# A megakernel's last expert group: weighted blocks added into two DRAM sums by accumulating indirect DMAs, with its down weights resident

## The reference, cut to what matters

```python
topk_idx, tw = _route(x, router_w, bias)                    # 4 of 16 experts for each token
combine = (one_hot(topk_idx, E) * tw[..., None]).sum(1)
y = jnp.einsum('etf,efd->etd', silu(x @ gate_w) * (x @ up_w), down_w)
routed = jnp.einsum('etd,te->td', y, combine)               # the weighted sum of a token's 4 rows
sh = silu(x @ sh_gate_w) * (x @ sh_up_w) @ sh_down_w        # two shared experts
x = x + tanh(g_ffn[1]) * (routed + sh)
```

## Time and profile before

| | us |
|---|---|
| median of the 3 runs (1596.46 to 1602.15) | 1599.17 |
| the profiled execution's own time | 1602.94 |
| its span, first to last instruction | 1601.1 |
| PE busy | 1303.0 (81%) |
| ACT busy | 1082.0 (68%) |
| DVE busy | 974.2 (61%) |
| POOL busy | 528.5 (33%) |

### The profile page before, as it was taken

How to read it: one execution, slowest core, us unless ns; L and a number is a source line. 1 busy time by engine, 2 the same in 40 slices (tenths; PEclk the granted TensorE clock), 3 DMA queues, 4 the chain that set the end, 5 groups by cost and what they waited for, 6 DMA issues and landing times.

```text
span 1601.1 us, 34625 instructions
## 1 busy us (share of the span) xinstructions
PE 1303.0 (81%) x11876; PEld 762.8 (48%) x11876; DVE 974.2 (61%) x2365; ACT 1082.0 (68%) x1781; POOL 528.5 (33%) x505
## 2 busy tenths in 40 slices
PE   6766777886789899988999899889997886888860
PEld 2211231352236554745475546544666575577650
DVE  7985466438843965498438864886467775223323
ACT  4999788967597799976987897768882431222220
POOL 1100111131553212326543445246424334503216
PEclk8987997988899999999999999999998997899985
DMA  7665403310122433453444554434346545579964
GB/s 210 217 197 119 86 1 95 77 53 27 67 86 61 132 95 78 116 124 107 139 109 123 146 148 111 133 97 149 95 126 189 147 119 147 165 192 232 257 171 119
DMA packets 228148, 202.55 MB, mean 127 GB/s; under 512 B 117099, under 2 KB 185875, under 8 KB 227987
## 3 DMA queue, kind: packets, MB, share of 16 engines
q1 hardware_dynamic: 203731, 155.24, 36.3%
q0 software_dynamic: 12288, 33.57, 6.5%
q10 hardware_dynamic: 11968, 11.54, 2.2%
HBM read 107.49 MB, written 67.63 MB: 109 GB/s over the span
## 4 chain that ended last, share of the span: by engine, by line
PE 45%; DVE 21%; ACT 21%; issue 7%; POOL 4%; DMA 1%; another core or an unknown queue 1%; POOLq 0%; SPq 0%; ACTq 0%; DVEq 0%
ACT tanh_tiles L1217 17%; PE psF L989 7%; PE psE L835 6%; PE psE L837 5%; PE psE L836 5%; PE psY L835 3%; PE psY L837 2%; PE psY L836 2%; PE psF L835 2%; POOL work L821 2%; DVE stats L1394 1%; PE psF L1156 1%; PE psF L837 1%; PE psF L841 1%; PE psF L836 1%
## 5 line engine op out<-in xcount | busy, mean ns | idle before, releaser
L1217 ACT ACTIVATE tanh_tiles<-feat,text_bias 128x512 f32<-128x512 f32 x1232 | 774.7, 714 | 76.6 <-DVE feat L1590 58.6
L989 PE MATMUL psF<-tanh_tiles,wslide 128*32 128x512 f32 x2464 | 374.5, 667 | 60.7 <-ACT tanh_tiles L1217 57.7
L1619 DVE TENSOR_TENSOR tile<-tile,psE 128x512 f32<-128x512 f32 x128 | 87.5, 684 | 159.8 <-ACT tile L1244 76.9
L768 POOL TENSOR_TENSOR hid<-tile,hid 128x512 f16<-128x512 f32 x76 | 88.4, 1163 | 251.2 <-ACT hid L1236 250.0
L821 POOL TENSOR_TENSOR work<-work 128x512 f16<-128x512 f32 (+1 forms) x80 | 95.5, 1197 | 228.0 <-DVE work L1756 228.0
L1236 ACT CAST hid<-tile 128x512 f16<-128x512 f32 x128 | 78.6, 614 | 133.5 <-DVE tile L1619 116.5
L792 POOL DMA_INDIRECT xs_rows<-xs,slot_i x128 | 127.2, 993 | 118.2 <-issue 32.0
L835 PE MATMUL psY<-down,hid 128*128 128x256 f16 x512 | 143.7, 281 | 18.4 <-issue 11.6
L836 PE MATMUL psE<-xg,up_hi 128*128 128x128 f16 x768 | 148.1, 222 | 9.5 <-issue 9.2
L837 PE MATMUL psE<-xg,up_lo 128*128 128x128 f16 x768 | 147.6, 221 | 9.7 <-issue 9.5
L835 PE MATMUL psE<-xg,up_hi 128*128 128x128 f16 x768 | 148.2, 221 | 6.9 <-issue 5.9
(11 more groups left out here) (302 smaller groups left out, 2880.9 us busy)
## 6 DMA issues: line engine op xcount, KB each, us to landing
down<-down_split SPq DMA_DIRECT2D x208, 256.0 KB
y_rows<-hid SPq DMA_DIRECT2D x52, 256.0 KB
xs_rows<-peakT SPq DMA_DIRECT2D x24, 512.0 KB, 6.8
y_rows<-tanh_tiles ACTq DMA_DIRECT2D x44, 256.0 KB
down_split<-hid SPq DMA_DIRECT2D x18, 256.0 KB, 3.4
xscan<-in_x SPq DMA_DIRECT2D x8, 512.0 KB, 5.2
x<-in_x SPq DMA_DIRECT2D x8, 512.0 KB, 5.4
w_lin<-w_split SPq DMA_DIRECT2D x15, 256.0 KB
```

The lines of the kernel that those rows point to most:

```text
L768: pool.tensor_tensor(hid_lo[:, n], tile[:, v.n % 2], hid_hi[:, n], ALU.subtract).then_inc(glo_done, 1)
L989: last = pe.matmul(psF[32 * j:32 * j + 32, RHO, :], wslide[:, c, 31 - g:63 - g], tanh_tiles[:, st.at(SETS, 2 * g + c) % HRING, j], start=g ...
L1217: act.activation(tanh_tiles[:, n % HRING, j], feat[:, c], ACT.Tanh, bias=text_bias[:, c, col:col + 1]).then_inc(h_ready, 1)
L1619: dve.tensor_tensor(tile[:, n], tile[:, n], psE[:, (2 * v.n + 1) % 3], ALU.mult).then_inc(g_done, 1)
```

## The change

It concerns group 3, the last one (`LASTG`), and nothing else of the arithmetic.

- The scattered rows become 1,120 bytes wide (`WIDE`): the two halves, the token's number and its 16 expert weights. They go to a DRAM table of their own, `xs_last`, which SP fills in steps 3 to 6 with empty rows that carry the number of one of 128 spare rows. Two sums in DRAM (`sums`, 1,152 rows of 256 fp32) are zeroed in step 7.
- One slot after a unit's start SP loads the numbers and weights of its 256 rows (`meta`). DVE picks, for each row, the weight of the block's owner (three small instructions, `wrow`).
- The copy of psY into the ring becomes two ACT instructions of 256 columns, scaled by `wrow`. The store to `y_rows` is gone.
- Instead, POOL adds block 0 of the unit into `sums[0]` 11 slots after the unit's start and block 1 into `sums[1]` one slot later, each with an indirect DMA that accumulates. Each waits for the one before into the same sum to have landed.
- At the end SP loads both sums in 8 DMAs of 256 KB, DVE adds them to `x` in 8 instructions of 512 columns, and SP stores 4 pieces. The 32 gathers and their weighted adds are gone.
- The down weights of the 16 experts are loaded once into SBUF (`resident`, 16 DMAs of 256 KB, step 9, slots 14 to 29), over buffers that the front part no longer needs. The 48 loads of a unit's own are gone; the down products now address `resident` by register.

```diff
+                if s == STEPS + 1 and 14 <= i < 14 + 1 * E and (i - 14) % 1 == 0:
+                    e = (i - 14) // 1
+                    if e == 0:
+                        sp.wait_ge(ids_ready, GROUPS)
+                        sp.wait_ge(slots_ready, GROUPS)
+                    sp.dma_start(resident[:, e].rearrange("p a k d -> p (a k d)"), down_dram[e]).then_inc(resident_loaded, 16)
...
             run(None, slot)
-            for c in range(CHUNKS):
-                sp.wait_ge(added, (GROUPS - 1) * CHUNKS + c + 1)
-                sp.dma_start(ov[2 * GROUPS - 2 + c // NT][:, c % NT], x[:, c // NT, c % NT]).then_inc(final_stored, 16)
+            sp.wait_ge(added, LASTG * CHUNKS)
+            for b in range(2):
+                sp.wait_ge(summed[b], 16 * NPAIR)
+            for q in range(4):
+                for b in range(2):
+                    rows = sums[b][2 * q * P:2 * (q + 1) * P].rearrange("(n p) c -> p n c", p=P)
+                    sp.dma_start(part[b][:, 2 * q:2 * q + 2], rows).then_inc(part_loaded[q], 16)
...
+                for b in range(2):
+                    v = began(T, STORE + b)
+                    if v and v.routed and v.g == LASTG:
+                        pool.wait_ge(y_kept, v.kept)
+                        if v.pair:
+                            pool.wait_ge(summed[b], 16 * v.pair)
+                        else:
+                            pool.wait_ge(last_filled, 16 * (PIECES + 2))
+                        keep_pace(i, s)
+                        pool.indirect_dma_start(sums[b], bass.IndirectOffsetOnAxis(ap=token_ids(v, b), axis=0),
+                                                y_rows(v)[:, b * D:(b + 1) * D], None, compute_op=ALU.add).then_inc(summed[b], 16)
...
             run(None, slot)
-            for m, count in enumerate(group_stored(GROUPS - 1)):
-                pool.wait_ge(y_stored[m], count)
-            for c in range(CHUNKS):
-                gather((GROUPS - 1) * CHUNKS + c)
...
+                cut = [slice((2 * b + f) * P, (2 * b + f + 1) * P) for f in range(2)]
+                if not v.entries:
+                    e = owners[v.n][b]
+                    wd = [[resident[:, bass.ds(e, 1), a, f].rearrange("p o d -> p (o d)") for f in range(2)] for a in range(2)]
...
+                        act.wait_ge(w_ready, v.pair + 1)
+                        for b in range(2):
+                            cols = slice(b * D, (b + 1) * D)
+                            last = act.activation(y_rows(v)[:, cols], psY[:, v.bank % 2, cols], ACT.Copy,
+                                                  scale=wrow[:, v.pair % META, b:b + 1])
```

More of the change, by code:

```diff
@@ L78 @@
 GROUPS = STEPS // 2
+LASTG = GROUPS - 1
 CHUNKS = 2 * NT
@@ L153, in plan @@
         v.n = n
-        if v.routed:
+        if v.routed and v.g < LASTG:
             v.entries = (entries, entries + 1)
@@ L184 @@
 UNITS, FREED = plan()
+assert all(v.late for v in UNITS if v.routed and v.g == LASTG)
 FIRST_LATE = min(v.n for v in UNITS if v.at >= LATE)
@@ L1245, in slot @@
                 v = began(T, STORE)
-                if v and v.late:
+                if v and v.late and v.g < LASTG:
                     act.wait_ge(y_kept, v.kept)
@@ L1608, in slot @@
                     add_shared(v, 1)
+                v = began(T, LOW + 1)
+                if v and v.routed and v.g == LASTG:
+                    n = v.pair % META
+                    dve.wait_ge(meta_loaded[n], 16 * (v.pair // META + 1))
+                    if v.pair:
+                        dve.wait_ge(w_ready, v.pair)
+                    if v.pair >= META:
+                        dve.wait_ge(y_kept, OF_R[v.r - META].kept)
+                    for b in range(2):
+                        block_at = 2 * v.pair + b
+                        last = dve.scalar_tensor_tensor(out=wsel[:, b], in0=iota[:, 0:E], scalar=owner_all[:, block_at:block_at + 1],
+                                                        in1=rows_gw(v, b), op0=ALU.is_equal, op1=ALU.mult)
+                    sw.link(last)
+                    dve.tensor_reduce(wrow[:, n], wsel[:, :, :], AX, ALU.add).then_inc(w_ready, 1)
                 v = began(T, LOW)
@@ L1774, in _ @@
             run(prelude, slot)
-            for c in range(CHUNKS):
-                n = (GROUPS - 1) * CHUNKS + c
-                dve.wait_ge(rows_got[buffer(n)], 16 * (gathers_before(n) + TOPK))
-                add_rows(x[:, c // NT, c % NT], rows_ring[buffer(n)], GROUPS - 1, c).then_inc(added, 1)
+            for q in range(4):
+                dve.wait_ge(part_loaded[q], 32)
+                mine = x[:, q // 2, 2 * (q % 2):2 * (q % 2) + 2]
+                ad.link(dve.tensor_tensor(mine, mine, part[0][:, 2 * q:2 * q + 2], ALU.add))
+                dve.tensor_tensor(mine, mine, part[1][:, 2 * q:2 * q + 2], ALU.add).then_inc(added, 1)
 INPUTS = ["x", "ctx_1024", "mask_BxS2_ik0", "g_xattn", "g_ffn",
```

155 lines of the change are left out of this document (119 added, 36 removed).

## The result

The changed kernel takes 1609.32 us (median of 11 runs, 1602.74 to 1614.54) against 1598.92 for the kernel before in the same series. The ratio is 1.0068 (95% interval 1.0054 to 1.0082), so the change costs 10.9 us. It leaves out one execution of the kernel before that fell out of the row with 1879.22 us. The forecast was 1606 against 1599.17, 7 us slower, with a range of 1576 to 1628.

What follows compares the result with a forecast made beforehand. Bounds: a matmul-free tail set by POOL's 32 gathers, before it PE's instruction stream, with POOL's indirect DMAs stopping other engines. Span 1601.1 - 26 + 13 + 20 = 1608, or 1606 us against the 1599.17 median; range 1576 to 1628.

Steps and rivals of the forecast that it cites:

- falls as a whole: Condition voiding the prediction: the scatter of wider rows or the loads of step 9 delay group 3's first unit.
- The tail: Last copy to kernel end: gathers go, accumulates, sum loads, adds and a store replace them; 26 us less, ends 31 and 16.
- the chain of accumulates behind the last copy: In the tail: accumulates into one sum follow each other, the third waiting for two landings; 3.3 us taken for each.
- The estimate by the Trainium skill: For tail accumulates: 2.0 us plus bytes at 436 GB/s, 2.3 us for 128 KB; tail ends 2 to 3 us earlier.
- Down weights by register: On PE in group 3: 8 register instructions in each of 24 units, 0.55 us a unit, 13 us more; bounds 9 and 28.
- The 16 loads: Step 9: 4.2 MB beside a stretch with DMA 43% busy, put at 0, at 5 if a transposing load gets late.
- 48 accumulates on POOL: Beside group 3's units: runs of four become six, 2.5 us for each of 8, 20 us more; bounds 0 and 28.
- Edits at nothing: Wider scatter, fills, DVE's small instructions, ACT's second copy, SP's row-number load: 0; SP's costs only if POOL falls 12 us behind.
- C: Rival: pauses come from full DMA engines, not POOL, and vanish, with register work at its lower bound; 1572 us, chance 0.08.
- A: Rival: added DMAs do not lengthen the pauses, POOL never issuing more than four in a row; 1586 us, chance 0.24.
- B: Rival: an accumulate takes longer than a unit, deciding from 5.9 us; at 7 us it gives 1625 us, chance 0.12.
- The rule of the Trainium skill that was told with C: All issuers share 16 engines; where a DMA is issued matters only for the issuer's own time, so POOL's issuing stops nobody.

Runs made afterwards that it cites:

- Q: Chip of the first follow-up series (ring of down weights, no accumulates, fixed addresses, loads spread); the kernel before takes 1563 us on it.
- R: Chip of the second follow-up series; kernel before again 0.9998, changed kernel again 1.0086 (1575.6 us); the kernel before takes 1563 us on it.
- no accumulates: Changed kernel without its 48 accumulating DMAs, so group 3's routed part is missing from the output; 0.9892 of the kernel before.
- no gathers: Changed kernel without the 32 gathers of group 2's chunks beside group 3's units, so that routed part is wrong; 0.9996 of the kernel before.
- the last kernel of S: Three sums, group 2's chunks from 8 slots earlier, one in 8 slots, down weights resident and addressed by register; 1.0056 of the kernel before.
- S: Chip of the third follow-up series, in which POOL's work was spread; the kernel before takes 1598 us on it.
- the spread kernel with the ring: Changed kernel with down weights loaded per unit into the ring, three sums, group 2's chunks 8 slots earlier, one in 8 slots; 0.9997 of the kernel before.
- the first chip: Chip of the blind prediction's measurement: changed kernel 1.0068 of the kernel before, 1609.32 against 1598.92 us.
- the ring: Changed kernel with each group 3 unit's down weights loaded into the ring again, no resident loads or register instructions; 1.0139 of the kernel before.
- three sums over the ring: Changed kernel with down weights in the ring again and accumulates taking three sums in turn instead of two; 0.9987 of the kernel before.

## Why the prediction was right, and where it was not

The sign and the size were right: 7 us slower forecast, 10.9 measured. It was right in good part by luck, because its misses offset each other. Its own text says that it falls as a whole if the loads of step 9 delay group 3's first unit. They did, by 7.5 us that the sum has at nothing. The tail came out 2.9 short and the registers 4.1 dearer, and the pauses, 12.5 cheaper than forecast, hid nearly all of it. With the runs on Q and R, where nothing pauses, the terms can be set apart. The split between registers and pauses depends on their order, as the two items on them say:

- **The tail**, forecast -26, measured -23.1 (57.8 us from the last silu to the end became 34.7). The mechanism was right. Mis-sized was the chain of accumulates behind the last copy: 9.3 us forecast and 14.5 measured (1584.54 to 1599.06). Three units' blocks were waiting, as forecast, but each link takes 4.5 us from start to start instead of 3.3: 3.6 to 3.8 to land and 0.7 to 1.0 until the next one starts. And the last unit's second block is issued 1.87 behind its first. The loads took 8.3 instead of 10.8. The estimate by the Trainium skill of 2.3 us for each such DMA, which the prediction set beside its sum, would have missed by more: the trace has 3.35 to 3.84. The same page (the Trainium skill, "DMA: Bandwidth & Descriptors", Two DMAs through the same engine are not ordered) asks for exactly this wait: only the completion semaphore says that a DMA has landed. Here it costs the landing time at each link of the chain.
- **Down weights by register**, forecast +13, measured +17.1: 140.4 us for the silus in the two runs where nothing else disturbs the register units (no accumulates on Q, no gathers on R), against 123.3. The mechanism was right, and the clean units are at 6.2 instead of the forecast 5.9. Beside pauses the same instructions cost 5.2, by the last kernel of S. The term, 0.55 a unit, was near the gap's growth (0.49) and left out that the gate loses its head start (0.2 to 0.3).
- **The 16 loads**, forecast 0 and 5 at most, measured +7.5, and 7.3 and 8.2 in the runs with and without them on R and S. This is the step that failed. It rested on a DMA share of 0.43 in one slice of 5 us, but the loads are issued from 1369 to 1405, and in the stretch from 1377 to 1409 the kernel before has a share of 0.70 already (its row of the table by stage is below). After it is 0.92, and a down load that group 2 waits for takes 7.58 us. PE idles 6.1 us for it and then runs 2 us longer at the lower level of the clock.

```profile
1377.00:1409.00 32.00, 29.63 (x262) 21.60 (x261) 11.70 (x17) 10.46 (x19) 11.70 (x12) 0.97 0.70 187
```

- **48 accumulates on POOL**, forecast +20, measured +7.5 (157.0 less 140.4 is 16.6 of pauses, 132.4 less 123.3 is 9.1 before). The runs came as foretold and mostly longer, 7 and 8 with one of 6, and ACT's idle time before five silus is about the 7.5 us forecast. In or behind five of the eight the clock fell to its lower level, the case that the forecast kept for its upper bound of 28 us; by the estimate above that is 4 to 7 of the 7.5 us. The price in the spread kernel with the ring, whose down products read fixed buffers, is 3.2 a chunk, near the 3.7 of the forecast (1.2 + 2.5). But beside register units it is 2.1. The step that was off is the addition of the two terms. Taken in the other order, the pauses cost 16.5 (148.9 less 132.4) and the registers 8.1 (157.0 less 148.9); only their sum, 24.6 against 33 forecast, is measured without such a choice. No run took the accumulates away on a chip with pauses.
- **Edits at nothing.** The price of an accumulate on POOL, 1.87 us, was taken as a gather's 1.25. On the first chip that was covered; on a chip without pauses it is what binds. SP's wait for row numbers stayed free with resident weights and was dear with the ring.

Sum: 2.7 + 7.5 + 17.1 + 7.5 - 23.1 = 11.7, of which the 2.7 are not explained: the two profiles are 3.0 us apart already at the silu at 513, and I did not follow that up. It is one profile of each kernel, and executions of the changed kernel lie up to 12 us apart, so a term is good to a few us.

Of the rivals, C (full DMA engines make the pauses) falls: at a share of 1.03 chip R shows none, and at 0.80 the changed kernel on the first chip shows longer ones. A (the pauses do not lengthen) falls too on the first chip. B has a true core that its condition hid. It asked for 5.9 us in one accumulate, and those in the chain take 3.35 to 3.84. But on R POOL's accumulates, gathers and waits for landings together fill some 146 of the 157 us, and without the gathers 14 us go. The rule of the Trainium skill that was told with C, by which the issuing engine matters only for its own time, agrees with this stage on chips Q and R and not with the first and S.

That makes the final account. On a chip with pauses the change loses by loads, registers and pauses. On one without, it loses by loads and by POOL's backlog, which covers the registers. Both give the same percent: 1.0068 and 1.0086. 48 accumulates of 1.87 us are 90 us of POOL work inside the stage, and they replace 40 us of gathers behind it. No kernel of the study that computes the whole output beat the one before; the best, three sums over the ring, is level with it.

## What to carry to other kernels

Before work moves from a bare tail into a busy stage, add up the issuing engine's own time there, waits for landings included: here 130 us of issue and some 15 of waits went into a stage of 132. Read the cover of a moved load over its whole stretch, not in one slice. When a wait grows, look at the granted clock behind it as well: its fall made part of the price in both stages here. And two slowdowns that fall on the same engine in the same stage need not add up; here their sum was the upper end.

## What the runs showed of the hardware

- An accumulating indirect DMA of 128 rows of 1,024 bytes into DRAM holds POOL for 1.87 us and lands 3.35 to 3.84 us after its start (in the chain at the end); a gather of the same bytes holds it 1.25.
- The medians of one program are 1563 us on two chips and 1599 on two others. On the first kind (Q, R) runs of four to eight indirect DMAs stopped neither PE nor ACT in group 3's units; on the other, runs of four cost 1.1 us a chunk, and longer ones 2.1 to 3.2 with the lower clock. The program was the same. The reason was not found.
- Behind waits that left PE idle or nearly so, the granted clock fell to its lower level: down matmuls 0.21 us apart instead of 0.11 at 1404.75, where PE had idled 6.1 us, and 128-column ones 0.11 apart instead of 0.06 at 1504.8, where it had got 7 matmuls done from 1500 to 1503. In the eight pauses of the kernel before it stayed at its upper level (1.00 over the silus of group 3, 0.95 after).
- Four register instructions more for each block's six matmuls cost 0.8 us a unit, 0.5 of it in the gap before the second block (1.07 instead of 0.58) and 0.2 to 0.3 in the gate that follows (1.67 instead of 1.35 to 1.47).
